# Routing an attention and expert kernel in two parts: nine token tiles during attention, thirty beside the first expert tiles

## What is computed

```python
h = _layernorm(x) * (1 + cb) + sb
expert_idx = jnp.argmax(h @ Wr.T + br, axis=-1)
y = relu(h @ W1[e].T + b1[e]) @ W2[e].T + b2[e]     # e = expert_idx of the token; hidden width 1024
x = x + gb * y
```

## Time and profile before

| what | value |
|---|---|
| median of 3 runs | 453.95 us |
| the profiled execution's own time | 455.38 us |
| its span in the trace | 453.3 us |
| busy in the span: TensorE (PE) | 427.4 us, 94% |
| VectorE (DVE) | 373.5 us, 82% |
| ScalarE (ACT) | 336.1 us, 74% |
| GpSimd (POOL) | 260.5 us, 57% |
| mean granted TensorE clock | 0.986 |

### The profile page before, as it was taken

One profiled execution on the slowest core, in us unless ns is written; L12 is line 12 of the kernel. 1 busy time (PEld: TensorE's weight loads), 2 busy tenths in 40 slices (PEclk: granted clock), 3 DMA queues, 4 the chain that ended last, 5 costly groups with the idle time before them and its releaser, 6 DMA issues.

```text
span 453.3 us, 14515 instructions
## 1 busy us (share of the span) xinstructions
PE 427.4 (94%) x4729; PEld 383.4 (85%) x4729; DVE 373.5 (82%) x1006; ACT 336.1 (74%) x853; POOL 260.5 (57%) x427
## 2 busy tenths in 40 slices
PE   6999899999999999958799999999999999999993
PEld 3988788898898888834379999999999999999992
DVE  2877999999999999889768877787777777788863
ACT  1557789899999998948177777777777777777770
POOL 2032577777767777674555666666666666664332
PEclk9999999999999999998899999999999999999997
DMA  8724455555555674120141212222221222100000
GB/s 279 263 94 140 149 176 163 169 162 165 163 165 169 179 247 142 48 82 23 48 122 48 72 52 73 70 70 70 65 71 56 71 64 65 51 26 25 21 18 2
DMA packets 23447, 46.90 MB, mean 103 GB/s; under 512 B 4683, under 2 KB 17228, under 8 KB 21200
## 3 DMA queue, kind: packets, MB, share of 16 engines
q1 hardware_dynamic: 17424, 31.82, 21.9%
q0 software_dynamic: 4992, 12.60, 9.3%
q10 hardware_dynamic: 960, 1.57, 1.0%
HBM read 35.22 MB, written 13.50 MB: 107 GB/s over the span
## 4 chain that ended last, share of the span: by engine, by line
PE 52%; DVE 36%; issue 6%; DMA 2%; ACT 2%; POOL 1%; DVEq 0%; ACTq 0%; POOLq 0%
PE ps_o L1583 22%; PE ps_va L1562 11%; PE ps_qk L1562 11%; DVE w L966 5%; DVE arena L1074 4%; DVE arena L1067 3%; DVE st L1077 2%; DVE arena L1101 2%; DVE arena L865 2%; PE ps_k L1300 2%; DMA w<-in_wmod 2%; DVE logits L1090 2%; DVE arena L1059 2%; DVE st L778 1%; DVE arena L1095 1%
## 5 line engine op out<-in xcount | busy, mean ns | idle before, releaser
L1583 PE MATMUL ps_o<-w,arena 128*128 x912 | 106.0, 273 | 0.2 <-issue 0.2
L1583 PEld LDWEIGHTS ps_o<-w,arena 128*128 128x128 f16 x912 | 87.5, 98 | 10.1 <-issue 0.5
L1215 DVE COPY w<-w 128x2048 f16 x78 | 60.9, 782 | 31.7 <-PE ps_qk L1562 29.0
L702 ACT ACTIVATE arena<-ps_qk,arena 128x128 f32<-128x128 f32 x156 | 44.5, 368 | 47.0 <-PE ps_qk L1562 47.0
L558 POOL DMA_INDIRECT out_rows<-arena,slot_token x39 | 46.2, 1185 | 33.8 <-POOL arena L552 30.7
L1201 DVE TENSOR_TENSOR arena<-arena 128x512 f16<-128x512 f32 x78 | 53.7, 688 | 10.1 <-ACT arena L710 9.9
L1562 PE MATMUL ps_qk<-arena,w 128*128 128x128 f16 x936 | 58.6, 219 | 0.6 <-DVE w L1215 0.6
L1562 PE MATMUL ps_va<-arena,w 128*128 128x128 f16 x936 | 58.6, 219 | 0.2 <-ACT arena L702 0.2
L552 POOL TENSOR_TENSOR arena<-arena 128x256 f32<-128x256 f32 x38 | 27.5, 722 | 51.8 <-DVE arena L1289 51.8
L1562 PEld LDWEIGHTS ps_qk<-arena,w 128*128 128x128 f16 x936 | 55.4, 98 | 2.0 <-issue 0.8
L1562 PEld LDWEIGHTS ps_va<-arena,w 128*128 128x128 f16 x936 | 55.4, 98 | 0.8 <-DVE w L1215 0.4
(11 more groups left out here) (230 smaller groups left out, 867.6 us busy)
## 6 DMA issues: line engine op xcount, KB each, us to landing
w<-in_w_raw SPq DMA_DIRECT2D x16, 1024.0 KB, 5.4
token_rows<-arena SPq DMA_DIRECT2D x64, 128.0 KB, 2.6
arena<-in_x SPq DMA_DIRECT2D x32, 128.0 KB, 2.3
b_sb<-in_b2b SPq DMA_DIRECT2D x1, 1024.0 KB, 5.6
w<-in_wmod ACTq DMA_DIRECT2D x1, 768.0 KB, 8.6
w<-in_wqkv SPq DMA_DIRECT2D x1, 768.0 KB, 8.3
arena<-token_rows,slot_token POOLq DMA_INDIRECT x39, 3.5
out_rows<-arena,slot_token POOLq DMA_INDIRECT x39, 2.7
```

Of the source, the lines that this page charges most:

```text
L702: last = act.activation(hid[:, f, :], bank[("qk", "va")[h]][:, (f % 4) * P:(f % 4 + 1) * P], ACT.Relu, bias=consts_now[:, r, f:f + 1], sca ...
L1215: dve.tensor_copy(now[:, :, i * F // 2:(i + 1) * F // 2], of[:, :, i * F // 2:(i + 1) * F // 2]).then_inc(s_w1, 1)
L1583: last = pe.matmul(bank[f"o{n % 2}"][:, 0:D], hid_parts[:, r % 2, b, f, :], w[:, bass.ds(m, 1), a, f * D:(f + 1) * D].rearrange("p a d -> ...
```

## The change

**Token order.** `row_of`, `in_rows` and `from_rows` lay the rows out in memory so that the rows of the first 16 chunks (`NA`) are the first 2048 rows. A gather of an early tile then reads only rows that the first 16 chunks have stored.

**Early part.** From the first 16 chunks, only full tiles are made: `TA` = 16 - 8 + 1 = 9 tiles. VectorE's routing operations are spread over the attention slots 21 to 29 (`early_route_1`, `_2`, `_3`, three places in each slot). TensorE computes the ranks in slot 22 and the token numbers after slot 31's projection. POOL makes the 16 marks in slots 28 to 31.

**Hand-over.** VectorE reads the token numbers in slot 32 (`early_tokens`), splits the last two pieces of matrix 14 there, and in slot 33 runs `first_tile`: it splits matrix 15, copies the first weights and splits the first tile's tokens, all ahead of the logits of chunks 29 to 31. ScalarE splits matrix 15 in slots 32 and 33 and tile 0 at the head of slot 34. POOL issues the first two gathers in slot 33, then the tile constants. The fillers on TensorE go from 63 matmuls to 14.

**Late part.** The other `TB` = 30 tiles come from all 32 chunks, with tokens already placed counted out. VectorE's work goes into the expert slots 0 to 3 and 6, POOL makes 24 marks (`POOL_MARKS`) in slots 3 to 5 and multiplies 960 columns once, ScalarE makes 8, and TensorE runs the 32 small matmuls after the second layer of tile 4. Nine buffers of scratch move to memory that is free by then; `tok` becomes a list of eight places.

```diff
+NA = NCH // 2
+TA = NA - NE + 1
+TB = NT - TA
+MARKS = 4
+POOL_MARKS = 24
@@ POOL
+            def mark_slots(of, numbers, i):
+                for n in range(i * MARKS, (i + 1) * MARKS):
+                    last = pool.tensor_scalar(of[:, n, :], slot_no16, numbers[:, n:n + 1], None, ALU.is_equal)
+                last.then_inc(s_bits, 1)
+            def first_gathers():
+                for b in range(B):
+                    pool.wait_ge(s_sx[b], 16 * (NA // B))
+                    pool.wait_ge(s_sh[b], 16 * (NA // B))
+                pool.wait_ge(s_x1, NCH - 4)
+                pool.wait_ge(s_tokens, 1)
+                gather(0)
+                gather(1)
@@ POOL, slot
+                if 0 <= (i := 2 * k + u - (NCH - MARKS)) < MARKS:
+                    pool.wait_ge(s_minus, 1)
+                    mark_slots(in_slot_a, slot_a, i)
...
+                if (k, u) == (NCH // B, 1):
+                    first_gathers()
+                    tile_constants()
             slots(pool, *ATT, slot)
+            pool.wait_ge(s_x1, NCH)
+            for n in range(2, 4):
+                gather(n)
+                constants_of(n)
             for b in range(B):
                 pool.wait_ge(s_sx[b], 16 * (NCH // B))
                 pool.wait_ge(s_sh[b], 16 * (NCH // B))
             pool.wait_ge(s_lgr, NCH)
+            for n in range(4, 6):
+                gather(n)
+                constants_of(n)
+            def gathered_in(s):
+                if s < TA - 6:
+                    return range(6 + s, 7 + s)
+                if s < TA - 3:
+                    return range(0)
+                if s < TA:
+                    return range(TA + 2 * (s - TA + 3), TA + 2 * (s - TA + 3) + 2)
+                return range(s + 6, min(s + 7, NT))
+            for s in range(NT + 1):
+                for n in gathered_in(s):
+                    if n == TA:
+                        pool.wait_ge(s_tokens, 2)
+                    gather(n)
+                    if n == TA:
+                        pool.wait_ge(s_routed, 2)
+                    constants_of(n)
+                if TA - 6 <= s < TA - 3:
+                    i = s - TA + 6
+                    if i == 0:
+                        pool.wait_ge(s_minus, 2)
+                        pool.wait_ge(s_hot, 2)
+                        pool.tensor_tensor(in_tile, in_tile, code16.unsqueeze(2).to_broadcast([P, NCH, TB]),
+                                           ALU.mult).then_inc(s_numbers, 1)
+                    mark_slots(in_slot, slot_f, 2 * i)
+                    mark_slots(in_slot, slot_f, 2 * i + 1)
+                if s > 0:
...
@@ ACT
             def slot(k, u):
+                if (k, u) == (FULL + 1, 0):
+                    token_hi(0, 0)
@@ DVE
+                if routing:
+                    early_route_1(B * k + u)
...
+                if routing:
+                    early_route_2(B * k + u)
+                if (k, u) == (FULL, 0):
+                    early_tokens()
...
+                if (k, u) == (FULL, 0):
+                    lo_piece(k, u, 0)
+                    lo_piece(k, u, 1)
+                if routing:
+                    early_route_3(B * k + u)
                 h_lo(k, u)
...
+                if (k, u) == (FULL, 1):
+                    first_tile()
+            def first_tile():
+                for i in range(PIECES):
+                    lo_piece(NM + i // 2, 1 - i // 2, i % 2, last=True)
+                dve.wait_ge(s_wlo, NM)
+                dve.wait_ge(s_b2, 16)
+                level()
+                m = matrix_number(0)
+                copy_w1(m, 0, 0)
+                copy_w1(m, 0, 1)
+                token_lo(0, 0)
@@ DVE, expert slots
+                if (it := ffn_item(k, u, 0)) and it[0] == TA - 3:
+                    late_tokens()
...
+                if (it := ffn_item(k, u, 0)) and it[0] == 0:
+                    late_ranks()
...
+                    if n == 0:
+                        late_places()
+                    if n == 1:
+                        late_slots()
+                    if n == 2:
+                        late_matrices()
@@ PE
+                if B * k + u == NCH - 1:
+                    pe.wait_ge(s_ht, NCH)
+                    pe.wait_ge(s_hot, 1)
+                    for n in range(NA):
+                        if n % MARKS == 0:
+                            pe.wait_ge(s_bits, n // MARKS + 1)
+                        last = pe.matmul(bank["x"][:, 2 * P:2 * P + TA], in_slot_a[:, n, :], in_tile_a[:, n],
+                                         start=(n == 0), stop=(n == NA - 1))
+                    last.then_inc(s_ids, 1)
...
-            keep_busy("k", 30)
...
-            keep_busy("k", 27)
+            pe.wait_ge(s_kg, CARRIED)
+            keep_busy("k", 4)
...
+            keep_busy("k", 4)
             pe.wait_ge(s_routed, 1)
+            def late_numbers():
+                pe.wait_ge(s_numbers, 1)
+                for n in range(NCH):
+                    if n == POOL_MARKS:
+                        pe.wait_ge(s_act_bits, 1)
+                    elif n < POOL_MARKS and n % MARKS == 0:
+                        pe.wait_ge(s_bits, NA // MARKS + n // MARKS + 1)
+                    last = pe.matmul(bank["kv1"][:, 0:TB], in_slot[:, n, :], in_tile[:, n], start=(n == 0),
+                                     stop=(n == NCH - 1))
+                last.then_inc(s_ids, 1)
...
                         elif (i == 0 or n == 0) and (ahead := ffn_item(k, u, -AHEAD)):
                             transpose_tokens(*ahead)
+                    if n == 0:
+                        late_ranks()
+                        pe.wait_ge(s_gb_sb, 1)
...
+                    if n == TA - 5:
+                        late_numbers()
```

More of the change, by code:

```diff
@@ L65, with row_of, in_rows, from_rows @@
 B1_AT = GB_AT + DK * B
+def row_of(g, r):
+    half = NCH // B // 2
+    return ((r if g < half else 3 - r) * half + g % half) * P
+def in_rows(a):
+    half = S // 2
+    return np.concatenate([a[0, :half], a[1, :half], a[1, half:], a[0, half:]])
+def from_rows(a):
+    half = S // 2
+    return np.stack([np.concatenate([a[:half], a[3 * half:]]), a[half:3 * half]])
 def constants():
@@ new lines, in build @@
+        code_f = place[:, 216:216 + TB]
+        in_tile = rows_1[:, 0:NCH * TB // 2].bitcast(F16).rearrange("p (n t) -> p n t", t=TB)
+        count_i, full_i, full, upto_tile, first = (pick[:, i * NE:(i + 1) * NE] for i in range(5))
+        pos, pos_i, tile_i, slot_i = (pick[:, 40 + i * NCH:40 + (i + 1) * NCH] for i in range(4))
+        slot_f, tile_16 = pick[:, 168:168 + NCH], pick[:, 200:200 + NCH // 2].bitcast(F16)
+        tile_f, token_f, empty_f = (pick[:, 216 + i * TB:216 + (i + 1) * TB] for i in range(3))
@@ L560, in slot @@
                                             oob_is_err=False).then_inc(s_out[n % 4], 16)
-            slots(pool, *FFN, slot)
             for r in range(4):
@@ L1192, in _, with last_choice, late_ranks @@
-            dve.wait_ge(s_wlo, NM)
-            dve.wait_ge(s_idx, 1)
-            dve.wait_ge(s_b2, 16)
-            dve.wait_ge(s_gb_sb, 1)
+                if (k, u) == (FULL, 1):
+                    first_tile()
+            def last_choice():
+                for i in range(4):
+                    mark(choose(24, NCH, i))
+                choose(24, NCH, 4).then_inc(s_chosen, 1)
+            def late_ranks():
+                dve.wait_ge(s_h2, NCH)
+                dve.wait_ge(s_rank, 2)
+                hop(dve.tensor_tensor_scan(upto, within[:], bank["k"][:, NE * NCH:2 * NE * NCH], 0.0, ALU.mult, ALU.add))
+                mark(dve.tensor_tensor(place, bank["k"][:, 0:NE * NCH], upto, ALU.add))
+                hop(dve.tensor_scalar(count_i.bitcast(I32), upto[:, NCH - 1:NE * NCH:NCH], float(P - 1), None, ALU.add))
+                hop(dve.tensor_scalar(full_i.bitcast(I32), count_i.bitcast(I32), 7, None, ALU.arith_shift_right))
+                mark(dve.tensor_copy(full, full_i.bitcast(I32)))
@@ new lines, in late_places @@
+            def late_places():
+                level()
+                hop(dve.tensor_tensor_scan(upto_tile, con("ones")[:, 0:1].to_broadcast([P, NE]), full, float(TA),
+                                           ALU.mult, ALU.add))
+                hop(dve.tensor_tensor(first, upto_tile, full, ALU.subtract))
+                hop(dve.scalar_tensor_tensor(of_experts(place), by_expert(first, NCH), float(P), of_experts(place),
+                                             ALU.mult, ALU.add))
+                dve.wait_ge(s_chosen, 2)
+                mark(dve.tensor_tensor(place, place, chosen16, ALU.mult))
```

418 lines of the change are left out of this document (239 added, 179 removed).

## The result

The changed kernel took 469.51 us, the median of 4 runs (468.54 to 469.95), beside 453.88 us (453.69 to 455.54) for the kernel before on the same chip: a ratio of 1.0333, 95% interval 1.0304 to 1.0362. It is slower by 3.3%, outside the range forecast. The profiled execution has a span of 467.6 us against 453.3, so 14.3 us more.

What follows compares the result with a forecast made beforehand. VectorE and TensorE are full in attention, TensorE in the expert part; only the hand-over can win. -8.5 (hand-over) + 0.5 + 1.0 + 1.0 + 2.3 (late part) = -3.7 us from 453.95: 450.2, range 445.0 to 455.5.

Steps and rivals of the forecast that it cites:

- Attention: Early routing added in slots 21 to 29, on a full VectorE: 4.0 us longer, bounds 2 to 8 us.
- First tile: Hand-over: the chain through norms, scale and shift, gather 0 and transposes starts tile 0 at 216.6 against 227.96, 11.4 us earlier.
- Second and third tile: Hand-over: tile 1 waits for tile 2's late gather; tile 2 starts at 229.7 against 238.24, a gain of 8.5 us.
- the lower clock: First tiles: after idle time TensorE runs at half speed; if tile 1 pays 2.7 us too, 452.9 us; chance 0.08.
- Contention: Expert slots 3 to 5: POOL's work beside VectorE's copies slows them, adding 1.0 us (0 to 3).
- POOL's marks: Late numbers: one 128-column mark on POOL takes 0.30 us, between 0.22 and 0.47.
- rival D: Slower: if a mark on POOL takes 0.6 us, TensorE stands 9.5 us behind tile 4, 457.4 us; chance 0.12.
- The rule built on it: TensorE's stop for the late numbers behind tile 4 is 3m - 4.9 = 2.3 us, bounds 0 to 5.9.
- 3m: Time of POOL's three groups of eight late marks, each group m = 2.4 us.
- The sum: Whole kernel: -8.5 + 0.5 + 1.0 + 1.0 + 2.3 = -3.7 us, so 450.2 us; chance 0.45.
- VectorE's late work: Late routing in expert slots 0 to 3: VectorE may be 2.0 us late, reaches 2.45, so TensorE stops 0.5 us.
- The gather of tile 9: Issued at most 3 us after TensorE goes on, transposes due a tile later: it lands in time.

Runs made afterwards that it cites:

- the best version: Changed kernel with 8 late marks on POOL, 16 and the product on VectorE, gathers of tiles 2 and 3 first, early choice one place earlier: 457.85 us, ratio 1.0001.

## Why the prediction was wrong

**Attention** was forecast 4.0 us longer. VectorE's attend step of chunk 29, in slot 31, came 4.04 us later, and the last attention matmuls 4.4: right. The profile showed VectorE full, and its added work went straight to the time; the parts of the 4.0 were not measured one by one.

**First tile.** Forecast 216.6, measured 217.53. The chain named (norms, scale and shift, gather, transposes) was the right one, and the forecast 0.9 us short. The granted clock was low there, 0.61 from 216 to 220 us, and it hid behind the next wait as forecast.

**Second and third tile.** The wait for tile 2's gather was forecast and is there, 4.65 us. But the gather was issued at 222.22 and not at 220.2, and behind the wait 24 matmuls of tile 1 ran at the lower clock (2.66 us for 1.50), which I had given a chance of 0.08. Tile 2 started at 233.61 and not at 229.7: the gain was 4.6 us instead of 8.5. This step was 3.9 us too good. (Its terms, 2.1, 1.9 and 3.0 from 208.9, make 215.9 and not 216.2.)

**Contention** was forecast at 1.0 us for the tiles beside POOL's product and marks. In slot 4 alone the step from tile 4 to 5 was 9.3 us instead of 5.5. The product held VectorE's gate step for 2.51 us. Of the 3.8 us more, 2.8 went when the product moved to VectorE. 1.1 of it are 24 matmuls that ran at the lower clock behind the wait (2.63 us for 1.50), and with more fillers these went too.

**POOL's marks are the step that failed.** I took 0.30 us for one, between 0.22 and 0.47, and wrote rival D for 0.6 us with a chance of 0.12. A mark took 0.58 us with VectorE idle (8 in 4.66) and 0.77 on average over the 24. The rule built on it came near: by its terms, with 18.5 us for 3m, the stop would be 18.5 - 4.9 = 13.6 us. TensorE waited 9.8 and had arrived 3.8 us late from slot 4, together 13.6. That this fits to the tenth is luck: counted from the start of tile 2 the marks began at 14.4 us and not at 12.7, and TensorE arrived at 27.4 and not at 22.5. (The rule also holds 0.3 us that no term names: 25.5 less 23.5 is 2.0, not 2.3.) So the order of POOL's list and what waits for it were read rightly, and the price was off by a factor of about 2 to 2.6. After the wait tile 6 ran at the lower clock for part of its time, 2.3 us more, which the forecast lacked.

**The sum.** From tile 2 on the forecast adds 4.8 us; measured were 18.9: 1.3 in slots 2 and 3, 3.8 in slot 4, 11.5 in slot 5 (the wait, the matmuls and 0.4), 2.3 in slot 6. With the start's 3.9 the miss at tile 8 is 18.0 us: 3.9 from the start, 0.8 from slots 2 and 3, 2.8 from slot 4, 8.2 from slot 5 and 2.3 from the clock in slot 6. The marks are the largest part and not the whole: rival D's 457.4 falls short, and with 18.5 us for 3m the forecast's own sum would still give only 461.5.

**VectorE's late work** was forecast at 0.5 us, from a copy that ends 2.1 us before its use; the rows give 2.45 (268.25 + 0.69 to 271.39), and by them it would have been about nothing. In the changed kernel slots 2 and 3 lost 1.3 us; what VectorE's work cost later couldn't be told, as VectorE had time while TensorE waited for POOL. In the best version the slots 2 to 5 lose 5.2 us, of which 1.2 are the number matmuls. There VectorE also has the product and 16 marks, 3.6 us more than in the change; how much the change's own part would cost alone was not separated.

**The gather of tile 9** was forecast to land in time. In the changed kernel it did, behind the slow tile 6; in the best version TensorE waited 1.82 us for it.

What would make this order win: tile 2 starts 6.6 us earlier and the late routing costs 9.3 us up to tile 10, so the price of the late part would have to fall below the gain. Shifting work between the engines didn't reach that. Of the 9.3 us, 5.2 are in slots 2 to 5, 0.8 in slot 6, 2.0 in slot 7, which has the wait for tile 9's gather, and 1.3 in slots 8 and 9, whose cause is open.

## What to carry to other kernels

Price an operation on POOL by rows of the same width on POOL, and take the dearest of the bounds where many of them stand one behind the other ahead of a wait: the number of repeats multiplies the error. Here even the dearest bound, 0.47 us, was below the 0.58 that a mark took at the least, because no row had the mark's form. Work moved "beside" a full stretch needs spare time on its engine slot by slot, not on average: VectorE's idle 19% in the expert part (17.88 of 22 us busy) is about 1.0 us a slot, its own list left 1.4, and 2.8 us put into one slot came out as a stop. An edit that removes a wait is worth what stands next in line; moving the product off POOL was worth 0.3 us with the marks behind it and 1.3 us without.
